# A fused 5x5/3x3 and quadratic convolution: the odd pixels of group 0 in another tile, the 3x3 shifts added first, a new order on VectorE, border corrections on diagonal tiles

## What is computed

```python
def reference(x, w3, b3, w5, b5, wr, br, filters):      # x: (8, 32, 64, 64)
    # _gn: every channel of every image on its own, (v - mean) / sqrt(var + 1e-5)
    x = x + conv0(_gn(x), ...)      # conv 5x5 and nine shifts of a zero-padded conv 3x3, weighted by wr, + br
    x = x + conv1(_gn(x), filters)  # per pixel: 9 taps per channel and a one, all pairwise products, times filters
    return x

# conv0
y3 = conv(x, w3, "SAME") + b3;  y5 = conv(x, w5, "SAME") + b5
P = pad(y3, 1)
shifts = [P[:, :, 2 - sw:2 - sw + H, 2 - sh:2 - sh + W] for sh in range(3) for sw in range(3)]
out = einsum('bcghw,cg->bchw', stack([y5] + shifts), wr) + br
# conv1
spot = concatenate([ones, patches3x3(x)])               # 10 values per channel and pixel
feat = (spot[..., :, None] * spot[..., None, :])        # 100 products
out = einsum('bcyxf,ocf->boyx', feat, filters)
```

## Time and profile before

| | before |
|---|---|
| median of three runs | 333.46 us |
| the profiled execution, its own time | 334.25 us |
| its span | 332.5 us |
| mean granted clock of TensorE | 0.975 |
| busy: TensorE, VectorE, ScalarE, GpSimd | 296.0, 203.2, 99.2, 39.7 us |

### The profile page before, as it was taken

The page is one execution under the profiler, slowest core; times in us unless marked ns, Lnnn a source line. Parts: engine busy times, 40 slices in busy tenths (PEclk is TensorE's granted clock), DMA queues, the critical chain, the costliest instruction groups (busy, mean ns, idle before and its releaser), DMA issues.

```text
span 332.5 us, 14548 instructions
## 1 busy us (share of the span) xinstructions
PE 296.0 (89%) x6976; PEld 148.7 (45%) x6976; DVE 203.2 (61%) x172; ACT 99.2 (30%) x150; POOL 39.7 (12%) x97
## 2 busy tenths in 40 slices
PE   0677956859999999999999999999999999999990
PEld 0123412345344745445647355644734554645550
DVE  1879719996297200999999955376005298883021
ACT  3521000597805899003200040882000000000091
POOL 3599980000000000100000000000000000000000
PEclk9999995978999999999999999999999999999998
DMA  6944000000000000000000000353000000000047
GB/s 199 371 104 101 4 1 2 2 2 5 2 2 2 6 2 4 2 4 2 4 2 4 4 4 2 67 118 77 4 2 2 4 4 2 4 3 4 4 97 158
DMA packets 7626, 11.51 MB, mean 35 GB/s; under 512 B 5392, under 2 KB 5520, under 8 KB 7440
## 3 DMA queue, kind: packets, MB, share of 16 engines
q1 hardware_dynamic: 5104, 9.59, 10.8%
q10 hardware_dynamic: 2464, 1.01, 1.3%
HBM read 6.40 MB, written 4.19 MB: 32 GB/s over the span
## 4 chain that ended last, share of the span: by engine, by line
PE 76%; POOL 11%; DVE 6%; issue 3%; ACTq 1%; ACT 1%; DVEq 0%; POOLq 0%
PE acc L771 64%; PE acc L798 9%; POOL folded L359 3%; POOL folded L339 3%; PE acc L848 2%; POOL sums L385 2%; DVE stats L630 1%; DVE product L549 1%; POOL sums L372 1%; ACTq L284 1%; DVE filters_in L576 1%; DVE filters_in L586 1%; DVE product L582 1%; POOL folded L342 0%; DVE plane L646 0%
## 5 line engine op out<-in xcount | busy, mean ns | idle before, releaser
L771 PE MATMUL acc<-product,weight 32*32 32x512 f32 (+1 forms) x4416 | 181.9, 597 | 0.0
L705 DVE TENSOR_TENSOR product<-plane 128x4096 f32<-128x4096 f32 x24 | 104.9, 4421 | 60.6 <-PE acc L771 37.0
L771 PEld LDWEIGHTS acc<-product,weight 32*32 32x32 f32 (+1 forms) x4416 | 95.3, 111 | 83.2 <-issue 60.4
L451 ACT ACTIVATE raw<-acc,offset_by_strip 32x512 f32<-32x512 f32 x36 | 24.5, 679 | 99.6 <-PE acc L771 99.1
L798 PE MATMUL acc<-product,middle 32*64 32x512 f32 (+1 forms) x576 | 30.3, 622 | 11.3 <-DVE product L577 6.9
L429 ACT ACTIVATE raw<-product 32x512 f32<-32x512 f32 x48 | 32.3, 674 | 0.7
L771 PE MATMUL acc<-plane,weight 32*32 32x512 f32 (+1 forms) x512 | 26.1, 599 | 0.0
L798 PEld LDWEIGHTS acc<-product,middle 32*64 32x64 f32 (+1 forms) x576 | 10.5, 128 | 30.8 <-issue 20.2
L669 DVE TENSOR_SCALAR raw<-acc,offset_by_strip 32x512 f32<-32x512 f32 x12 | 9.1, 757 | 24.0 <-PE acc L771 23.7
L630 DVE BATCH_NORM_STATS2 stats<-raw 128x6 f32<-128x512 f32 x32 | 19.7, 680 | 3.2 <-DMA raw<-in_x 3.2
L549 DVE TENSOR_TENSOR product<-plane 128x2048 f32<-128x2048 f32 (+1 forms) x8 | 18.7, 2370 | 0.0
(11 more groups left out here) (89 smaller groups left out, 164.7 us busy)
## 6 DMA issues: line engine op xcount, KB each, us to landing
raw<-in_x SPq DMA_DIRECT2D x8, 512.0 KB, 8.7
out<-raw SPq DMA_DIRECT2D x12, 256.0 KB, 2.9
filters_in<-in_L_conv_filters SPq DMA_DIRECT2D x4, 400.0 KB, 3.9
out<-product SPq DMA_DIRECT2D x8, 64.0 KB, 2.5
out<-product ACTq DMA_DIRECT2D x8, 64.0 KB, 2.7
w_in<-in_L_conv_w ACTq DMA_DIRECT2D x4, 100.0 KB, 4.1
w_in<-in_L_conv_w ACTq DMA_DIRECT2D x2, 36.0 KB, 1.9
w_in<-in_L_conv_w SPq DMA_DIRECT2D x2, 36.0 KB, 2.2
```

The source lines that it names most:

```text
L451: last = nc.scalar.activation(strip_rows(g, r, s, h), strip_acc(s, h, r), ACT.Identity, bias=offset_by_strip[32 * s:32 * s + 32, r, g:g + 1])
L705: nc.vector.tensor_tensor(product_rows(n), inner(g, 0, H), shifted(g, PRODUCTS[k]), ALU.mult)\
L771: return nc.tensor.matmul(acc[32 * s:32 * (s + strips), h, r, :], weights[32 * r:32 * r + 32, t:t + strips, :] .rearrange("p t c -> p (t c ...
```

## The change

1. **The odd half of group 0** is kept in `product[2]` instead of over the filters, so `whole_and_cross(0)` no longer waits for the sums. To make room, "left" of group 1 moves behind "step" of group 0 in `product[0]` and its borders are cleared by VectorE, once part three of group 0 is done. The borders of all product buffers are now cleared after part eight.
2. **Taps.** GpSimd clears `folded` and adds the nine shifts first. ScalarE scales the 5x5 taps in place; GpSimd adds them last, column by column (3, 4, their sum, then 0, 1, 2), behind the clearing of the halved planes' borders. ScalarE makes `half_one` and `minus_one` (`copy_taps`) instead of VectorE.
3. **VectorE's order**: `statistics(1)` and `whole_and_cross(0)` before "right"; the ring and the edge weights behind `normalise(1)`; `normalise(2)` ahead of `finish_even(1)`; the odd pixels of the last image of group 0 are spread by VectorE (`spread_last`).
4. **Border corrections**: side `side` of image r goes to column tile (r + side) % 4 instead of r, so its results lie in other partitions and `copy_edges` evicts them in 13 pieces instead of 4. In group 1, `edges0(0)` comes behind both forms of "next".

```diff
-            buf = product[((0, 1), (3, 2))[g][name in ("left", "right")]]
-            return (buf, SECOND_AT, HALVES[name][2]) if name in ("step", "right") else (buf, 0, HALF_W)
+            place = {"total": (0, 3), "step": (0, 3), "left": (1, 0), "right": (1, 2)}[name][g]
+            second = name in ("step", "right") or (name == "left" and g == 1)
+            return product[place], SECOND_AT if second else 0, HALVES[name][2]
...
-            return filters_in[:, 0:GROUP * CHUNK] if g == 0 else product[1][:, 0:GROUP * CHUNK]
+            return product[(2, 1)[g]][:, 0:GROUP * CHUNK]
...
-            pool.wait_ge(taps5_ready, 1)
+            nc.gpsimd.memset(folded[:, :, :], 0.0).then_inc(shift_folded, 1)
+            pool.wait_ge(shift_folded, 1)
...
-                pool.wait_ge(shift_folded, n + 1)
-                if n == 5:
+                pool.wait_ge(shift_folded, n + 2)
+            for g in range(NG):
+                for name in ("total", "step", "left", "right"):
+                    if (g, name) != (1, "left"):
+                        pad_half(g, name).then_inc(padded, 1)
+            pool.wait_ge(taps5_ready, 1)
+            for n, x in enumerate((3, 4, 0, 1, 2)):
+                part = folded[:, 5 * x:5 * x + 5, :]
+                nc.gpsimd.tensor_tensor(part, part, w5_in[:, :].rearrange("p (c y x) -> p x y c", y=5, x=5)[:, x, :, :],
+                                        ALU.add).then_inc(columns_added, 1)
+                if n == 1:
+                    pool.wait_ge(columns_added, 2)
                     nc.gpsimd.tensor_tensor(folded[:, PAIR_AT:PAIR_AT + 5, :], folded[:, 15:20, :], folded[:, 20:25, :],
-                                            ALU.add).then_inc(columns_added, 1)
+                                            ALU.add).then_inc(pair_added, 1)
...
             for n in range(PRODUCT_BUFS):
-                g = n // 2
-                pool.wait_ge(part_done, 4 * (g + 1))
-                if n == 1:
-                    pool.wait_ge(odd_spread, GROUP * NG)
+                pool.wait_ge(part_done, 4 * NG)
+                if n in (0, 3):
+                    pool.wait_ge(even_spread, GROUP * (n // 3 + 1))
                 else:
-                    pool.wait_ge(even_spread, GROUP * (g + 1))
+                    pool.wait_ge(odd_spread, (2 * GROUP - 1, GROUP - 1)[n - 1])
+                    pool.wait_ge(odd_taken, 1)
...
+            def copy_taps():
+                act.wait_ge(outer_turned, 1)
+                nc.scalar.activation(half_one[:, :, :], weight0[:, 5:10, :], ACT.Copy, scale=0.5).then_inc(taps_copied, 1)
+                nc.scalar.activation(minus_one[:, :, :], weight0[:, 15:20, :], ACT.Copy, scale=-1.0)\
+                  .then_inc(taps_copied, 1)
...
                 for side, b in enumerate((18, 16, 21, 19)):
-                    last = nc.scalar.activation(edges[:, g, side, :], acc[:, 1, side, 0:W], ACT.Identity,
-                                                bias=ring_bias[:, b:b + 1])
+                    for r in range(GROUP):
+                        s = (r + side) % STRIPS
+                        if side == 0:
+                            if r == 0:
+                                nc.scalar.activation(edges[:, g, side, :], acc[:, 1, side, 0:W], ACT.Identity,
+                                                     bias=ring_bias[:, b:b + 1])
+                        else:
+                            last = nc.scalar.activation(edges[32 * r:32 * r + 32, g, side, :],
+                                                        acc[32 * s:32 * s + 32, 1, side, 0:W], ACT.Identity,
+                                                        bias=ring_bias[32 * s:32 * s + 32, b:b + 1])
...
             normalise(0)
+            copy_taps()
             keep_whole(0)
             std(1)
             normalise(1)
             spread(0, 0, range(GROUP))
             copy_edges(0)
-            spread(0, 1, (0, 1))
             keep_whole(1)
-            spread(0, 1, (2, 3))
+            spread(0, 1, range(GROUP - 1))
...
-                if g == 0:
-                    dve.wait_ge(sums_ready, 1)
...
             halve(0, "step")
             halve(0, "left")
+            step(statistics(1, wait_piece(1), every))
+            whole_and_cross(0)
             halve(0, "right")
-            make_ring()
-            turn_edges()
             dve.wait_ge(far_padded, 1)
             halve(0, "far")
-            add_constants()
-            whole_and_cross(0)
-            last = statistics(1, wait_piece(1), every)
+            normalise(1)
             finish_even(0)
-            normalise(1, last)
             middle_taps(1)
             halve(1, "total")
+            turn_edges()
+            make_ring()
+            finish_odd(0)
             halve(1, "step")
-            finish_odd(0)
+
+            buf, at, pitch = half_at(1, "left")
+            dve.wait_ge(part_done, 3)
+            nc.vector.memset(buf[:, at:at + 2 * pitch], 0.0)
+            nc.vector.memset(buf[:, at + (LINES - 2) * pitch:at + LINES * pitch], 0.0)
             halve(1, "left")
+            spread_last(0)
+            add_constants()
             turn_filters()
             halve(1, "right")
+            whole_and_cross(1)
             halve(1, "far")
-            whole_and_cross(1)
             finish_x1(0)
-            last = statistics(0, lambda n: None, every)
+            step(statistics(0, lambda n: None, every))
+            normalise(2)
             finish_even(1)
-            normalise(2, last)
             finish_odd(1)
...
-                            nc.tensor.matmul(acc[32 * r:32 * r + 32, 1, side, 0:W],
+                            s = (r + side) % STRIPS
+                            nc.tensor.matmul(acc[32 * s:32 * s + 32, 1, side, 0:W],
                                              weight0[32 * r:32 * r + 32, EDGE_AT + 5 * side + t + 2, :], pixels,
-                                             start=t == -2, stop=t == 2 and side >= 2, tile_position=(32 * r, 32 * r))
+                                             start=t == -2, stop=t == 2 and side >= 2, tile_position=(32 * r, 32 * s))
...
-            product0(1, "next", 0, True, False, False)
+            product0(1, "next", 0, True, False, True)
+            product0(1, "next", 0, False, False, False)
+            edges0(0)
             product0(1, "total", 0, False, False, False)
-            edges0(0)
-            product0(1, "next", 0, False, False, True)
             product0(1, "total", 0, False, True, True).then_inc(part_done, 1)
```

More of the change, by code:

```diff
@@ L161, in conv_kernel @@
         columns_added = sem("columns_added")
+        pair_added = sem("pair_added")
+        taken_over = sem("taken_over")
         pair_ready = sem("pair_ready")
-        outer_ready = sem("outer_ready")
+        outer_turned = sem("outer_turned")
+        taps_copied = sem("taps_copied")
         padded = sem("padded")
@@ L326, in pad_half @@
                 return nc.gpsimd.memset(buf[:, at + (LINES - 2) * pitch:at + LINES * pitch], 0.0)
-            for g in range(NG):
-                for name in ("total", "step", "left", "right"):
-                    pad_half(g, name).then_inc(padded, 1)
-            pool.wait_ge(taps5_ready, 1)
+            nc.gpsimd.memset(folded[:, :, :], 0.0).then_inc(shift_folded, 1)
+            pool.wait_ge(shift_folded, 1)
             five = folded[:, 0:TAPS0, :].rearrange("p (x y) c -> p x (y c)", x=5)
@@ L487, in _ @@
             act.wait_ge(taps3_ready, 1)
-            scale_shifts(range(3))
+            scale_shifts(range(len(EY_EX)))
             act.wait_ge(taps5_in, 64)
-            nc.scalar.activation(folded[:, 0:TAPS0, :].rearrange("p (x y) c -> p x y c", x=5),
-                                 w5_in[:, :].rearrange("p (c y x) -> p x y c", y=5, x=5),
-                                 ACT.Copy, scale=wr_in[:, 0:1]).then_inc(taps5_ready, 1)
-            scale_shifts(range(3, len(EY_EX)))
+            nc.scalar.activation(w5_in[:, :], w5_in[:, :], ACT.Copy, scale=wr_in[:, 0:1]).then_inc(taps5_ready, 1)
             std(0)
@@ L553, in outer_taps @@
             def outer_taps():
-                dve.wait_ge(shift_folded, len(EY_EX))
-                step(turn(0, TAPS0))
-                nc.vector.tensor_scalar(minus_one[:, :, :], weight0[:, 15:20, :], -1.0, None, ALU.mult)\
-                    .then_inc(outer_ready, 1)
-                step(nc.vector.tensor_scalar(half_one[:, :, :], weight0[:, 5:10, :], 0.5, None, ALU.mult))
+                dve.wait_ge(columns_added, 5)
+                turn(0, TAPS0).then_inc(outer_turned, 1)
+                dve.wait_ge(outer_turned, 1)
             def middle_taps(g):
@@ L631, in statistics, with normalise @@
                 return last
-            def normalise(phase, last):
+            def normalise(phase):
                 stage, g = divmod(phase, NG)
-                step(last)
                 step(nc.vector.bn_aggr(mean_var[:, :], stats[:, :, :].rearrange("p n s -> p (n s)")))
```

(27 more changed lines are left out.)

14 lines of the change are left out of this document (7 added, 7 removed).

## The result

The changed kernel takes 328.12 us (median of 4 runs, 326.79 to 329.23) against 333.45 beside it: ratio 0.984, 95% interval 0.982 to 0.986. It is faster, as forecast, but by 5.3 us and not 12.8, and outside the range of 317 to 324.5. The profiled execution took 326.79 us with a span of 325.1; the forecast for a span was 319.8.

A forecast was written before the change was run, and what follows sets the result against it. TensorE, busy 89%, bound the kernel: only less matmul work or fewer waits could shorten it. Span 332.5 - 18.5 + 4.0 = 318.0, with 1.8 for half clock 319.8, plus 0.96: 320.6 us in round terms; range 317 to 324.5.

The forecast's parts named there:

- Part 1, first weights: Filter taps at the start: "total" starts on TensorE at 24.55 us against 27.24, -2.7 us (-3.3 to -1.4).
- Part 2, the wait for the sums: TensorE's wait for `whole_and_cross(0)` goes, -6.9 us, and the clock doesn't fall behind it, -1.7 us.
- POOL's sums ... free: GpSimd's filter sums, wanted at 64.7 us and done at 48.3 before, cost nothing in spite of a later start.
- halvings ... (2.2 each): VectorE's halvings "right" and "far" of group 0 take 2.2 us each and end at 43.1 us.
- Part 3, the corrections: Group 1 and border corrections: TensorE's waits shrink, -5.2 us; corrections -1.8 us (0 to -2.1), 0.3 more from the clock.
- 160 x 17 = 2.7 us, and with the corners (0.5) 3.2: Border corrections of group 0 on TensorE: 160 records at 17 ns plus corners take 3.2 us instead of 5.0.
- Part 4, what comes late next: Fifth product behind part eight: ScalarE's chain +4.0 us, ready at 146.4, wanted at 141.6; TensorE stands for 4.7 us.
- The clock: one fall said: Behind TensorE's 4.7 us pause for the fifth product, restart at half clock costs 1.8 us (1.2 to 2.5).
- Weights late: Rival, 12%: VectorE blocks GpSimd's column additions, "total" starts 1.3 to 5 us later, time 322 to 326 us.
- Corrections not shorter: Rival, 15%: the new tiles don't shorten the border corrections, part eight is 1.7 us later, clock stays, time 320.6 us.

The follow-up runs named there:

- places alone: Kernel before plus only: odd pixels of group 0 in the product buffer, "left" of group 1 moved, borders after part eight, no wait for the sums: 327.17 us, ratio 0.980.
- old tiles: Changed kernel with the border corrections on column tile r for every side and four edge copies instead of 13: 321.79 us, ratio 0.965.
- second profiled execution: Changed kernel run again with nothing changed: median 327.62 us, ratio 0.983; its profiled execution took 325.56 us.
- the cut corrections: Changed kernel with the border corrections cut in two, long matmuls between the halves: 330.36 us, ratio 0.990.
- the fastest kernel: Changed kernel with corrections on column tile r, first buffer's borders after part seven, "right" before the statistics, edge weights and ring before "far": 318.73 us, ratio 0.956.

## Why the prediction was right or wrong

**Part 1, first weights: right.** "Total" starts at 25.32; 24.55 was said, 23.9 to 25.8 the range. A column addition took 0.60 us undisturbed (0.5 said); one that met a halving took 2.65.

**Part 2, the wait for the sums: right in itself; the step beside it failed in the profiled execution.** The wait of 6.9 us and the half clock behind it are gone; places alone gave 6.2 us with all that follows. But "POOL's sums ... free" and "halvings ... (2.2 each)" didn't hold. I had read that a VectorE operation with two inputs in SBUF holds GpSimd up (three shifts in 4.67 us) and took it for a one-way street. GpSimd's additions in an unbroken row can hold VectorE up just as well: 3.4 us in that execution, 2.7 with old tiles, nothing in the second profiled execution of the same kernel. In the kernel before, VectorE waited idle for the 21 sums, so only the other direction could be seen: the three sums ahead of them took 3.63 us beside "far".

**Part 3, the corrections: the rate was right; the term failed, and it is the one that the runs price highest.** 13.5 ns a record against 17 said and 15 as lower bound. By the rule of the Trainium skill (TensorE: Matmul & The Clock Gate, Part 3: Packing small matmuls, and Back-to-back issue gap) it should have stayed near 25 ns; the measurement decides against it for these tiles. The step that failed is "160 x 17 = 2.7 us, and with the corners (0.5) 3.2": the rate was read from a burst of 31 weight loads, and 192 loads with their matmuls run out of instructions. First record to next product took 3.9 us, not 3.2, and in group 1 5.1, no less than before (5.0). `finish_odd(0)` at 61.3 instead of 57.6 is the VectorE step above. Part eight ended at 93.4 instead of 89.0: 3.7 from where the corrections start, 0.7 from their stop.

**Part 4, what comes late next: the mechanism right, two sizes off.** The fifth product was decisive, as each run that moved the ScalarE chain shows (the cut corrections most of all). It came 58.8 us behind part eight, not 57.4: the copies took 4.1 us and not 3.0, since 32-partition copies started 0.317 us apart and did not overlap (my upper bound of 0.32), and the square started 0.58 behind part eight instead of 0.45. So 152.2 instead of 146.4: 4.4 + 1.1 + 0.1 and 0.2 of the spreads. TensorE's wait was 2.1 and not 4.7, because the stop and a half-speed stretch near 102 had made TensorE itself late: the same loss under other names. The rest of the program took 172.9 us (171.6 + 1.8 said). Sum: +5.8 - 0.5 = +5.3, the whole gap to the profiled span; the median lies 1.3 us above that execution.

**The second profiled execution** has no delay of the halvings, and its span of 323.8 us is still 4.0 over the forecast: the corrections start 0.8 late and take 4.1 us instead of 3.2, half clock behind their stop costs 1.5, the copies and the square 1.1, and the rest gains 0.3. So the halvings alone don't explain the miss. Diagonal tiles do explain most of it: they were forecast to gain 1.8 us in the corrections against 2.1 us in the copies, and taking them out gained 5.8 to 6.3.

**The clock: one fall said, two came** (each 3.4 us at half clock, so 1.7 lost; 1.8 said), and three in the second profiled execution (mean 0.982 in the first, 0.971 to 0.976 in the three runs beside it). The runs spread by 2.4 us, and by 3.3 us when run again, where the four of the kernel before spread by 0.2; but the kernel before, in 11 runs beside each set of experiments, spread by 1.7 to 2.1 us. What spreads the changed kernel's time isn't shown: in the six runs the fastest had one of the lowest mean clocks (0.976).

**The range** ended at 324.5. It held 1.5 us for VectorE's delays and nothing for a rival in which POOL holds up VectorE. "Weights late" had the right engine pair and the wrong direction. "Corrections not shorter" had a rate of 25 ns in mind and no stop. (319.8 and 0.96 make 320.8, where 320.6 was written; nothing hangs on it.)

## What to carry to other kernels

When a wait is removed that made one engine idle beside another, ask what those two do to each other once they run at the same time, in both directions; the profile of before may show only one. Put operations there that hardly compete (a transpose, a statistic). Profile a kernel more than once before a row of one execution becomes a rule. A rate read from a short burst is not the rate of a long row. And price what a faster layout asks of the engine that reads it out: here 0.5 us less in one set of TensorE's corrections, and 0.4 more in the other, cost 3.2 us on the chain that set the end.

## What the runs showed of the hardware

- Where GpSimd's additions of 32 to 96 elements, issued without a wait between them, met a VectorE tensor_tensor with both inputs in SBUF, one of the two waited. In three executions VectorE waited 3.3 to 3.4 us (5.63, 5.56 and 5.64 us instead of 2.25), with old tiles 2.7; in two of these four it got in ahead of the last additions, which then waited (11.48 us for the 21 instead of 7.28). In a fifth VectorE did not wait (2.31) and the additions took 12.73 us. What decides stays open.
- Beside the same additions, VectorE operations with one input in PSUM (2.29), statistics and transposes (0.97) were not slowed. Four copies of 32x512 within SBUF took 2.48 us beside the first three, and 1.74 alone; operations on one element with two inputs took up to 0.42 instead of 0.16.
- 64-column matmuls with their loads on sixteen 32x32 tiles in turn go at 13.5 to 15 ns a record, on four diagonal ones at 25, at full clock.
- TensorE's instructions came in packets of 16 KB, 259 in each, never less than 3.3 us from start to start. Amid the short matmuls TensorE stopped behind instruction 1985 or 3777 and went on 1.25 to 1.57 us after a packet had ended: for 0.8 to 2.1 us in each kernel with the sixteen tiles, for 0.7 us at most on four (0.56 and 0.69 in the fastest kernel, 0.35 in the kernel before).
- ScalarE's copies of 32x64 started 0.317 us apart, those of 128x64 0.21. Why they don't overlap stays open.
- Pauses of TensorE of 1.3 to 2.3 us could already be followed by half clock in these kernels (behind 99.5 to 101.4 us in one execution, 98.2 to 99.5 in the other), but were not always: the one of 59.2 to 61.4 in the changed kernel was not.
